# The front of a kernel's second half: another order for the last fold, the ffn tiles and the transposes between them

## The reference

```
x = L0_attn_hidden_states                       # (2, 512, 512)
sa, ca, ga, sb, cb, gb = modulation(L0_c, L0_wmod)
h = layernorm(x) * (1 + ca) + sa
x = x + ga * L0_attn(h)      # 32 heads, chunked linear attention, gated; @ Wo.T
h = layernorm(x) * (1 + cb) + sb
x = x + gb * L0_ffn(h)       # one product with a ternarised 512 x 512 weight
sa, ca, ga, sb, cb, gb = modulation(L1_c, L1_wmod)
h = layernorm(x) * (1 + ca) + sa
x = x + ga * L1_attn(h)      # 32 query heads of 16, 8 key heads, RoPE, softmax
h = layernorm(x) * (1 + cb) + sb
x = x + gb * L1_ffn(h)       # 4 streams mixed, 50 Sinkhorn iterations
```

## Time and profile before

| | |
|---|---|
| median of 3 runs | 1512.79 us (1510.37 to 1515.64) |
| the profiled execution | 1508.06 us |
| its span, first to last instruction | 1506.3 us |
| mean granted TensorE clock | 0.915 of full speed |
| TensorE busy | 1240.5 us, 82% |
| VectorE busy | 1007.1 us, 67% |
| GpSimd busy | 732.3 us, 49% |
| ScalarE busy | 622.7 us, 41% |

### The profile page before, as it was taken

The page is one execution under the profiler, slowest core; times in us unless marked ns, Lnnn a source line. Parts: engine busy times, 40 slices in busy tenths (PEclk is TensorE's granted clock), DMA queues, the critical chain, the costliest instruction groups (busy, mean ns, idle before and its releaser), DMA issues. The chain is left out here.

```text
span 1506.3 us, 18429 instructions
## 1 busy us (share of the span) xinstructions
PE 1240.5 (82%) x6008; PEld 876.0 (58%) x6008; DVE 1007.1 (67%) x1721; ACT 622.7 (41%) x1166; POOL 732.3 (49%) x740
## 2 busy tenths in 40 slices
PE   4889999999999999999999999876989998961000
PEld 2678767767776777777777777655753333430000
DVE  6746665565655566655655656666678888748898
ACT  2334333333433433334434433334517777753203
POOL 0456765656655756656656665675420012031107
PEclk9999999999999999999999999998979999985555
DMA  4211122122123121121221211130185310000001
GB/s 161 81 50 56 57 69 86 43 77 71 56 58 91 49 71 48 58 78 42 64 70 50 63 50 64 57 99 1 37 181 93 48 58 2 2 1 0 1 0 56
DMA packets 70488, 86.47 MB, mean 57 GB/s; under 512 B 6789, under 2 KB 40741, under 8 KB 69818
## 3 DMA queue, kind: packets, MB, share of 16 engines
q1 hardware_dynamic: 68138, 81.52, 19.6%
q10 hardware_dynamic: 2256, 3.77, 0.9%
HBM read 77.49 MB, written 7.51 MB: 56 GB/s over the span
## 5 line engine op out<-in xcount | busy, mean ns | idle before, releaser
L1473 ACT ACTIVATE yTh<-yF 128x512 fp32r<-128x512 f32 x64 | 40.4, 631 | 318.9 <-DVE yF L1045 318.9
L1692 POOL TENSOR_TENSOR sw<-sw,sinT 128x512 f32<-128x512 f32 x80 | 103.4, 1293 | 138.5 <-ACT sw L1424 138.5
L1207 DVE TENSOR_REDUCE nm<-banks 128x2 f32<-128x1024 f32 x128 | 151.2, 1218 | 25.8 <-PE banks L752 25.7
L1706 POOL TENSOR_TENSOR dec<-gb,gcol 128x512 f32<-128x512 f32 x64 | 70.6, 1104 | 195.4 <-DVE Sd L1011 191.3
L1584 ACT ACTIVATE Pb<-banks 128x512 f32<-128x512 f32 x256 | 135.0, 601 | 47.6 <-PE banks L773 47.3
L983 DVE SCALAR_TENSOR_TENSOR gs<-tg,banks 128x512 f32<-128x512 f32 x64 | 44.0, 687 | 118.6 <-ACT tg L1431 118.6
L547 PE MATMUL banks<-hTh,wgh 128*128 128x512 f32 x256 | 122.1, 477 | 0.0
L599 PE MATMUL banks<-st,qt 128*128 128x128 f32 x384 | 80.4, 293 | 37.1 <-DVE Sd L1011 21.1
L627 PE MATMUL banks<-woh,yTh 128*128 128x512 f32 x256 | 104.9, 410 | 3.5 <-DVE yTl L1048 3.5
L547 PE MATMUL banks<-hTh,wqh 128*128 128x512 f32 x256 | 106.3, 415 | 0.0
L627 PE MATMUL banks<-woh,yTl 128*128 128x512 f32 x256 | 101.5, 397 | 0.0
(11 more groups left out here) (310 smaller groups left out, 3269.3 us busy)
## 6 DMA issues: line engine op xcount, KB each, us to landing
gb<-g_scr SPq DMA_DIRECT2D x64, 256.0 KB, 3.4
raw<-in_wmod SPq DMA_DIRECT2D x40, 256.0 KB, 2.7
raw<-in_wg SPq DMA_DIRECT2D x32, 256.0 KB, 2.7
raw<-in_wo SPq DMA_DIRECT2D x32, 256.0 KB, 2.8
raw<-in_wq SPq DMA_DIRECT2D x30, 256.0 KB, 2.7
qsT<-q_scr SPq DMA_DIRECT2D x22, 256.0 KB, 6.9
q_scr<-hl SPq DMA_DIRECT2D x28, 128.0 KB, 4.6
mt<-mods_scr SPq DMA_DIRECT2D x12, 256.0 KB, 4.7
```

The lines of the kernel that those rows point to most:

```text
L1207: ve.tensor_reduce(nm[:, b, i, p:32:16], pairs[z_][:, :].rearrange("p (g t) -> p g t", g=2), AX.X, ALU.max, negate=True).then_inc(*v_nm.up ...
L1692: po.tensor_tensor(s_[:, :], s_[:, :], sinT[:, :], ALU.mult).then_inc(*g_rope.up("sin", kind, t, n))
L1706: po.tensor_tensor(dec[:, :, :], gb[s % 2][:, :, :], bc(gcol[:, t % 2, heads(t), n], 2, 128), ALU.subtract).then_inc(*g_dec.up("sub", s))
```

## The change

- `fold_b`, in all 64 slots, does the 8 matmuls with yTh first and waits only for yTh; then it waits for yTl and does the 4 matmuls with it.
- `ffn` of a batch's first tile and the k projection wait for each low part k by itself, just ahead of its matmuls. The projections of batch 0 wait for the weight parts that each bank needs.
- `turn_h` is split: VectorE's subtraction is a step of its own, `low_h`. `conv` is split into ScalarE's `conv` and VectorE's `conv_low`, and the v weights are now part 10, part 9 the second half of the k weights.
- In `last_folds` the last `fold_a` comes behind the first turn's transposes and ahead of its low part; the residuals of tiles 4 to 6 stand between the turns; the weight copies on ScalarE (8, 9, 10, 0 to 3) follow; the residual of tile 7 and all moments and norms of batch 1 stand ahead of ffn(0) to ffn(2).
- In `middle` the turns of batch 1 stand between ffn(2) and ffn(3), the four turns of batch 0's second norm between ffn(5) and ffn(6), and VectorE's low parts of the weights behind everything that the tiles need.

```diff
         def fold_b(self, s):
             pe = self.e
-            pe.wait_ge(*v_yl(s))
+            pe.wait_ge(*a_yh(s))
...
             for h in range(4):
-                hi, lo = wts["o", h]
-                for y_, w_ in ((yTh, hi), (yTh, lo), (yTl, hi)):
-                    mm = pe.matmul(banks[bO][:, :], y_[:, h, :], w_[:, :], start=(c == 0), stop=(c == 11))
-                    c += 1
+                for n, w_ in enumerate(wts["o", h]):
+                    pe.matmul(banks[bO][:, :], yTh[:, h, :], w_[:, :], start=(h == 0 and n == 0), stop=False)
+            pe.wait_ge(*v_yl(s))
+            for h in range(4):
+                mm = pe.matmul(banks[bO][:, :], yTl[:, h, :], wts["o", h][0][:, :], start=False, stop=(h == 3))
...
         def ffn(self, i, bk):
-            pe.wait_ge(*v_hl("f", i // 4, 3))
...
+            for k in range(4):
+                if i % 4 == 0:
+                    pe.wait_ge(*v_hl("f", b, k))
...
         def proj(self, b, u):
-            pe.wait_ge(*v_hl("a", b, 3))
-            if b == 0:
-                pe.wait_ge(*v_aw("k" if u == 2 else "q"))
             for n in range(2):
                 bk = bks[n]
+                if b == 0:
+                    pe.wait_ge(*(v_aw("k", n) if u == 2 else v_aw("q", 4 * n + 3)))
...
                 for k in range(4):
+                    if u == 2 and n == 0:
+                        pe.wait_ge(*v_hl("a", b, k))
...
     def turn(E, of, b, k, bk):
-        E.turn_h(of, b, k, bk, *E.spare((of, b, k)))
+        z_, prev = E.spare((of, b, k))
+        E.turn_h(of, b, k, bk, z_, prev)
+        E.low_h(of, b, k, bk, z_, prev)
...
     def last_folds(E):
...
-        turn(E, "f", 0, 0, E.bank())
+        first = ("f", 0, 0, E.bank(), *E.spare(("f", 0, 0)))
+        E.turn_h(*first)
+        E.fold_a(last)
+        E.low_h(*first)
         turn(E, "f", 0, 1, E.bank())
-        E.fold_a(last)
+        E.residual("f", 4)
         turn(E, "f", 0, 2, E.bank())
+        E.residual("f", 5)
         turn(E, "f", 0, 3, E.bank())
-        for i in (4, 5, 6):
-            E.residual("f", i)
-        E.conv(8), E.conv(9)
-        E.moments("f", 4)
+        E.residual("f", 6)
+        for part in (8, 9, 10, 0, 1, 2, 3):
+            E.conv(part)
         E.fold_b(last)
         E.loop_end()
-        E.moments("f", 5)
         E.residual("f", 7)
...
+        for i in range(4, 8):
+            E.moments("f", i), E.norm("f", i)
+        for i in range(3):
+            E.ffn(i, E.bank())
+
+    def middle(E):
+        E.bias(0, None)
+        E.conv_low(8)
+        turn(E, "f", 1, 0, E.bank())
+        E.moments("a", 0)
+        turn(E, "f", 1, 1, E.bank())
+        turn(E, "f", 1, 2, E.bank())
+        E.moments("a", 1)
+        turn(E, "f", 1, 3, E.bank())
         E.ffn(3, E.bank())
         for part in range(4, 8):
             E.conv(part)
+        E.norm("a", 0), E.norm("a", 1)
+        E.moments("a", 2), E.norm("a", 2)
+        E.moments("a", 3), E.norm("a", 3)
+        E.ffn(4, E.bank())
+        E.conv_low(9)
+        E.ffn(5, E.bank())
+        turn(E, "a", 0, 0, E.bank())
+        E.moments("a", 4)
+        turn(E, "a", 0, 1, E.bank())
+        E.moments("a", 5)
+        turn(E, "a", 0, 2, E.bank())
+        turn(E, "a", 0, 3, E.bank())
+        E.norm("a", 4), E.norm("a", 5)
+        E.ffn(6, E.bank())
+        E.conv_low(10)
+        E.memsets(0)
+        E.bias(1, E.bank())
+        E.ffn(7, E.bank())
+        for i in (6, 7):
+            E.moments("a", i), E.norm("a", i)
+        for part in range(8):
+            E.conv_low(part)
         E.memsets(1), E.key_ones(0)
```

More of the change, by code:

```diff
@@ L420, in build @@
         load_gb = start_loads = w_values = w_turn = residual = residual_most = residual_last = moments = norm = turn_h = ffn = load_mods = a_weights = scaled_rows = col_turn = nothing
-        memsets = proj = vproj = vturn = prod_u = comb = high = low = stow = stow_high = place_high = place_k = place_q = key_ones = tables = key_cols_ = conv = bias = pass_a = max_part = scores_b = pv = out1 = out2 = nothing
+        memsets = proj = vproj = vturn = prod_u = comb = high = low = stow = stow_high = place_high = place_k = place_q = key_ones = tables = key_cols_ = conv = conv_low = low_h = bias = pass_a = max_part = scores_b = pv = out1 = out2 = nothing
         r_loads = gates = square = rms = turn_l = logits = mix_y = scaled = pre = rest1 = rest2 = rest3 = nothing
@@ L654, in turn_h @@
             self.drain[bk] = a_hh("F", of, b, k)
[L656 to L662, removed]
         def ffn(self, i, bk):
-            pe = self.e
-            pe.wait_ge(*v_hl("f", i // 4, 3))
+            pe, b, c, sl = self.e, i // 4, 0, slice(i % 4 * 128, i % 4 * 128 + 128)
             if i == 0:
@@ L669, in ffn @@
             pe.wait_ge(*self.drain[bk])
-            self.by_token(i, fTh, fTl, 512, bk, i // 4).then_inc(*p_ffn.up(i))
+            for k in range(4):
+                if i % 4 == 0:
+                    pe.wait_ge(*v_hl("f", b, k))
+                for x_, w_ in ((hT2h[b], fTh), (hT2h[b], fTl), (hT2l[b], fTh)):
+                    mm = pe.matmul(banks[bk][:, :], x_[:, k, sl], w_[:, k, :], start=(c == 0), stop=(c == 11))
+                    c += 1
+            mm.then_inc(*p_ffn.up(i))
             self.drain[bk] = v_ffn(i)
@@ L1141, in ffn, with conv_low @@
             ve.tensor_tensor(xin[i][:, :], banks[bk][:, :], mt[0, 5, b][:, :], ALU.mult).then_inc(*v_ffn.up(i))
-        def conv(self, part):
+        def conv_low(self, part):
             ve = self.e
@@ L1522, in conv @@
                     ac.wait_ge(*p_o(NSLOT - 1))
-                ac.activation(inner(aqh[:, half, k, :]), wide(aqr[:, k, :])[:, half, :, :, :], ACTF.Copy).then_inc(*a_aw.up(part))
+                ac.activation(inner(aqh[:, half, k, :]), wide(aqr[:, k, :])[:, half, :, :, :], ACTF.Copy).then_inc(*a_aw.up("q", part))
             elif part == 8:
@@ L1526, in conv @@
                 ac.activation(kwh[:, 0, :, :, :].rearrange("p k h x -> p (k h x)"), kp[:, :, :, :].rearrange("p k h x -> p (k h x)"), ACTF.Copy).then_inc(*a_aw.up("k", 0))
+            elif part == 9:
                 for h in range(2):
-                    ac.activation(kwh[:, 1, :, h, :], kp[:, :, 1 - h, :], ACTF.Copy).then_inc(*a_aw.up("k", 1 + h))
+                    a = ac.activation(kwh[:, 1, :, h, :], kp[:, :, 1 - h, :], ACTF.Copy)
+                a.then_inc(*a_aw.up("k", 1))
             else:
@@ L1839, in key_ones @@
             if b == 0:
-                po.wait_ge(*v_aw("q"))
+                po.wait_ge(*v_aw("q", 7))
                 po.wait_ge(*g_vp("one", 1))
@@ L2217, in last_folds @@
+        for part in (8, 9, 10, 0, 1, 2, 3):
+            E.conv(part)
         E.fold_b(last)
         E.loop_end()
-        E.moments("f", 5)
         E.residual("f", 7)
-        E.ffn(0, E.bank())
-        E.norm("f", 4), E.norm("f", 5)
-        E.moments("f", 6)
-        E.ffn(1, E.bank())
-        E.norm("f", 6)
-        E.moments("f", 7)
-        E.ffn(2, E.bank())
-        E.norm("f", 7)
-        E.ffn(3, E.bank())
-    def middle(E):
-        E.moments("a", 0)
-        for k in range(4):
-            turn(E, "f", 1, k, E.bank())
-            if k < 3:
-                E.moments("a", k + 1)
-        for i in range(4):
-            E.norm("a", i)
-        E.bias(0, None)
-        E.ffn(4, E.bank())
-        turn(E, "a", 0, 0, E.bank())
-        turn(E, "a", 0, 1, E.bank())
-        E.ffn(5, E.bank())
-        E.moments("a", 4)
-        E.memsets(0)
-        turn(E, "a", 0, 2, E.bank())
-        E.ffn(6, E.bank())
-        E.moments("a", 5)
-        turn(E, "a", 0, 3, E.bank())
-        E.conv(0), E.conv(1)
-        E.bias(1, E.bank())
-        E.norm("a", 4), E.norm("a", 5)
-        E.ffn(7, E.bank())
-        E.moments("a", 6), E.norm("a", 6)
-        E.conv(2), E.conv(3)
-        E.moments("a", 7), E.norm("a", 7)
```

16 lines of the change are left out of this document (8 added, 8 removed).

## The result

The changed kernel's median is 1500.34 us (1500.02 to 1503.29, 5 runs), before 1511.82 us (1507.84 to 1515.64, 5 runs, with the three shown). The difference of the two medians is 11.5 us. The ratio, estimated from all runs, is 0.9928 with a 95% interval of 0.991 to 0.9946, which is 10.9 us less, 8.2 to 13.6. The profiled execution took 1500.28 us, its span is 1497.5 us.

What follows compares the result with a forecast made beforehand. The 58.4 us from the last transposes before the final fold to the first q projection were taken as bound by a chain through all engines. 13.8 less 1.3 and 0.5 gave 12.0 us gained: 1501 us, range 1497.5 to 1504, 73%.

Steps and rivals of the forecast that it cites:

- low clock: Behind the new standstill before the second batch's transposes: one slow piece of 1.7 us, partly hidden, 1.3 us off the gain.
- held products: VectorE products held by GpSimd additions and placed too well in the forecast: 0.5 us off the gain.
- signs that the prediction named: No wait for yTl, none of 5 us for hT2l, one of 3 to 4 us for hh; q projection near 1062.
- The last fold and ffn 0 to 2: Last fold ends at 1019.0 instead of 1023.7, 4.7 us earlier; ffn(2) ends at 1028.0 against 1031.9.
- The new standstill: TensorE stands still 3.65 us from 1028.0, until tile 7 is normalised and the second batch's transposes start at 1031.65.
- What took its place: Behind ffn(5), forecast starts: second norm's transposes 1043.7, ffn(6) 1047.1, ffn(7) 1050.4, 16 transposes behind the k projection 1058.6.
- Waits for each part: No term of its own; ffn(0), waiting for each low part, was to stand still 0.3 + 0.5 us.
- The loop's folds: The loop's 63 other folds: 0 taken, at most 0.03 us each, 2 us; as a rival 3%, 1503.
- Given back behind the stretch: Pass over the scores: 0 lost, at most 2 us in the forecast; as a rival 5 to 10 us, 5%.
- Half the gain: Rival, 15%: tile 7's chain 1.5 us late, two slow pieces, a norm delayed; gain 7.9 us, about 1505.
- the bank releases: Sharp edge of the half-gain rival: banks of ffn(0) to (2) given back only behind the moments, 1030.5 to 1031.7.
- Slower by low clock throughout: Rival, 4%: from the standstill at 1028 on, clock low through the middle, costing 19.8 us; 6 us slower, 1519.

Runs made afterwards that it cites:

- fold_only: The kernel before with only the changed fold_b, everything else in the old order: 1510.47 us (10 runs), ratio to before 1.0007.
- fold_old: The changed kernel with fold_b in the old order, waiting for yTl first: 1494.61 us (1 run).
- whole_waits: The changed kernel with the old whole waits in ffn and the projections instead of waits for each part: 1501.84 us (1 run).
- bias_late: The changed kernel with GpSimd's bias copies behind ffn(5) instead of at the start of middle: 1500.87 us (1 run).
- more_banks: The changed kernel with the turns of batch 1 and of batch 0's second norm in banks 3 to 6: 1497.41 us (1 run).
- tile4_early: The changed kernel with tile 4's residual and moments moved ahead, into slots 62 and 63: 1499.87 us (6 runs).
- three_moves: The changed kernel with the edits of tile4_early, more_banks and bias_late together: 1498.16 us (6 runs), ratio to before 0.9916.
- new_folds_old_middle: The changed kernel with its new last_folds, but ffn(3) in its old place and the old middle: 1502.22 us (9 runs), ratio to before 0.9962.
- old_folds_new_middle: The changed kernel with last_folds in the old order, less ffn(3), and the new middle: 1506.95 us (10 runs), ratio to before 0.9973.

## Why the prediction was right, and where it was not

The forecast was 1501, the median 1500.34. The gain in the stretch was computed as 13.8 less 1.3 for low clock and 0.5 for held products, 12.0; it is 11.9 from yn to q projection. The new order and the waits it removes came as computed; that the number came to 0.1 us is luck, as the points on the low clock and on what took its place show. That the total came within 1 us is luck as well, since runs of before lie 7.8 us apart. The signs that the prediction named came, except that the 16 transposes behind the k projection still wait, for 0.31 us. Point by point:

- *The last fold and ffn 0 to 2* came to within 0.2 us: fold at 1016.00 (1016.1), ffn(0) 1018.87 (1019.0), its parts at 1020.59 and 1021.79 (1020.6 and 1021.8), end of ffn(2) 1028.05 (1028.0). That fold_b waits for yTh alone, which I had in the same step, is worth nothing, as fold_only and fold_old show. So the gain of this step is left to yF and yTl ahead of the low parts (yF at 1014.53 instead of 1017.08); no run isolates that from the rest of last_folds.
- *The new standstill* was computed as 3.65 us and is 3.2, the transposes at 1031.43 (1031.65). The rest of the chain, ffn(3) at 1034.96 (1035.05), held too.
- *The low clock* is the step that failed. I took one piece of 1.7 us behind that standstill, 1.3 net. None came: the stretch has a clock of 1.00, and q - yn is the same in both traces of the changed kernel. The earlier trace rows should have warned me: after the 3.09 us wait ahead of 1039.02 the 12 transposes took 1.53 us, and 12 at full clock take 1.47 (1014.33 above). A slow piece is not bound to a wait of a given length: after 2.75 us in whole_waits one came, after 2.97 and 2.96 us at one place in the loop one and none. At the new standstill itself none came after 3.2 us in five traces (the changed kernel twice, fold_old, bias_late, more_banks), and one did after 2.2 us in tile4_early and 2.1 in three_moves. The second batch's 16 transposes in more_banks, tile4_early and three_moves, one row each:

```profile
1031.08 1.97 PE L652 MATMUL banks<-cst,hh 128*128 128x128 f32 x16 [3.20 <-ACT hh L1489]
...
1029.44 3.62 PE L652 MATMUL banks<-cst,hh 128*128 128x128 f32 x16 [2.16 <-DVE xin L1142]
...
1036.84 3.42 PE L652 MATMUL banks<-cst,hh 128*128 128x128 f32 x16 [2.14 <-ACT hh L1492]
```

  The granted clock over the 4 us from the second row's start is 0.58. Even so the slow piece cost nothing that lasted: from these transposes to those of the second norm it is 13.15 us in tile4_early and 13.12 in the changed kernel, 12.75 in three_moves and 12.76 in bias_late. So both parts of the term were wrong, that the piece comes and that it costs 1.3 us here. The Trainium skill (TensorE: Matmul & The Clock Gate, section "HAM oscillation — how this bites in real kernels") tells of a kernel in which every tile starts cold behind a DMA wait of about 3 to 5 us. The waits of 2.1 to 3.2 us here lie at or below the lower end of that, and behind them the rows show both outcomes.
- *What took its place* is 1.7 us of lateness behind ffn(5), 1.9 if counted from yn. The second norm's transposes came at 1044.55 instead of 1043.7. Half of this stands in VectorE's list already: I had the second batch's low parts done and the product of ffn(3) begun at 1038.9, and the product began at 1039.34. The chain from there to the transposes took 5.2 us instead of 4.75. GpSimd's copies (4.0 us from 1034.59) I had not priced; bias_late gets 0.4 us back, 0.1 of it in GpSimd's own list. Later steps were late by more: ffn(6) by 1.0 us (1048.09 for 1047.1), ffn(7) by 1.2 (1051.6 for 1050.4), the 16 transposes by 1.8 (1060.38 for 1058.6), for which TensorE still waits 0.31 us for tile 7's row. These I did not take apart. So the 12.0 was met by allowances of 1.8 us for things that did not come and 1.9 us of lateness that I had not seen.
- *Waits for each part* were priced inside the steps; alone they are 0.5 us.
- *The loop's folds*: 0, as taken.
- *Given back behind the stretch*: up to 2 was allowed. At the last v projection the profiled execution is 12.4 us ahead, at the first pass_a 11.0, at the end 8.8. The first 1.4 us are a longer wait for the placing by DMA: from the last v projection matmul to pass_a it is 2.6 us in before and 3.1 in fold_only, and 3.0 to 4.8 in the eleven traces with a new order, 3.8 on average. That hints at a loss of about 1 us by the new order, and I have no run that isolates it; the two traces of the changed kernel alone have 4.0 and 4.8. The other 2.2 us are within the 224 to 230 us that scores take from one trace to the next. The profiled execution of before lay 3.8 us under the median of its five runs (4.7 under that of the first three), that of the changed kernel 0.1 under its own. This is why the medians show 11.5 us and this pair 7.8 by its times and 8.8 by its spans.
- *The rivals.* Half the gain did not come. Of its edges the bank releases are real, but small: more_banks takes them away and gains 0.6 us. Slower by low clock throughout did not come either. The longest slow pieces seen in these stretches are some nine matmuls in new_folds_old_middle (from 1036.85 to 1040.2) and 16 transposes with three matmuls in old_folds_new_middle (from 1042.33 to 1047.7).

## What to carry to other kernels

Follow the chain through all engines, not TensorE's idle time: filling its 3.2 us standstill with ffn(3) cost 0.3 us, while taking 1.7 us of work off VectorE's list gained 1.9. When a chain is VectorE's, an order of calls matters by what stands ahead of the one operation that others wait for, and by what GpSimd does beside it, small copies included. Before you price a wait by the low clock behind it, check whether every such wait in your own rows brought it and whether another engine bounds what follows. For changes of a few us compare landmarks inside one execution (here they repeat to 0.1 us) and leave the total to many runs.

## What the runs showed of the hardware that I had not expected

Low clock behind a wait is a matter of the single execution. The same wait of 2.96 to 2.97 us at the same slot of the loop was followed by 1.2 GHz in some executions and by 2.4 GHz in others, a difference of 2.4 us in that slot and 3.1 from slot 54's yn to slot 63's (122.2 and 125.3 us). Most of what is left of the 6 us by which the last yn differs (1011.3 to 1017.2) is of the same kind. From the first yn to slot 15's it is 221.2 us in five traces and 224.4 in eight. The 3.2 us between them fall behind a wait of 3.97 us ahead of slot 1 (granted clock around it 0.93 or 0.87) and one of 2.96 us ahead of slot 9 (1.00 or 0.96 over slots 9 and 10). three_moves, whose last yn is at 1020.4, has 3.2 us more at slots 33, 41 and 42, and there too its clock is the lower one (0.86 for 0.93, 0.96 for 1.00).

Three GpSimd additions at 1030.47 beside VectorE work took 4.17 us, 0.42 more than the 3.75 of three at the pace of 1.25 us that one has alone, and one low part beside an addition 1.68 us instead of 0.68: the two engines' work with two operands in SBUF went one after the other. The Trainium skill (SBUF — State Buffer, section "Who interferes with whom") says that whoever is first blocks the other for a whole instruction. The 1.68 us agree with it: the addition begun at 1018.70 ended at 1019.99, and 0.68 us from there reach 1020.67, within 0.14 us of the low part's end at 1020.53.
